# Output projection kept in the PSUM bank of the weighing for its last eleven steps

## The reference, cut to what matters

```
x = x + attention(layernorm(x), wq, wk, wv, wo)    # 32 query heads, 8 key/value heads of 64, rope, causal
x = x + cross(layernorm(x), ctx)                   # fp8-rounded in blocks of 128, one product per batch
x = x + moe(layernorm(x), Wg, W1, W3, W2, shared)  # 8 experts, top 1, capacity 256, and a shared expert
```

## Time and profile before

| | |
|---|---|
| median of three timed runs | 1606.17 us (1605.36 to 1607.48) |
| profiled execution, its own time | 1609.08 us |
| its span | 1607.3 us |
| PE busy | 1460.3 us, 91% of the span |
| DVE busy | 1202.9 us, 75% |
| POOL busy | 1020.0 us, 63% |
| ACT busy | 949.2 us, 59% |
| the profiled steps 124 to 134 | from about 999 us to about 1079 us |

### The profile page before, as it was taken

The page is one execution under the profiler, slowest core; times in us unless marked ns, Lnnn a source line. Parts: engine busy times, 40 slices in busy tenths (PEclk is TensorE's granted clock), DMA queues, the critical chain, the costliest instruction groups (busy, mean ns, idle before and its releaser), DMA issues.

```text
span 1607.3 us, 26926 instructions
## 1 busy us (share of the span) xinstructions
PE 1460.3 (91%) x8616; PEld 1276.6 (79%) x8616; DVE 1202.9 (75%) x2951; ACT 949.2 (59%) x2384; POOL 1020.0 (63%) x1007
## 2 busy tenths in 40 slices
PE   5689899999998999999999998666989898899997
PEld 4468788888877888888888887556888887899996
DVE  6678688888877778877878878976767664687785
ACT  2367677877766687878877877523121213566662
POOL 1677688988966788888888877632313132344455
PEclk8899999999999999999999999897899999899998
DMA  5654243344332334334334433012010002577767
GB/s 195 179 157 148 61 116 112 85 120 125 81 104 50 78 86 126 91 93 120 99 93 112 110 79 109 14 55 86 27 27 27 7 27 97 175 232 224 229 215 236
DMA packets 106588, 177.04 MB, mean 110 GB/s; under 512 B 16662, under 2 KB 38422, under 8 KB 106448
## 3 DMA queue, kind: packets, MB, share of 16 engines
q1 hardware_dynamic: 103888, 167.07, 35.9%
q0 software_dynamic: 2560, 8.25, 1.6%
HBM read 97.28 MB, written 31.98 MB: 80 GB/s over the span
## 4 chain that ended last, share of the span: by engine, by line
PE 66%; DVE 15%; ACT 7%; issue 5%; POOL 3%; DMA 2%; SPq 1%; DVEq 0%; POOLq 0%; ACTq 0%
PE bank L411 14%; PE bank L412 14%; PE bank L413 14%; PE bank L453 6%; PE bank L429 4%; PE bank L468 4%; PE bank L469 4%; PE bank L430 4%; ACT P L756 3%; PE bank L403 2%; DVE P L1033 2%; DVE Opair L1068 1%; ACT xnx L778 1%; ACT Otmp L762 1%; DVE work L981 1%
## 5 line engine op out<-in xcount | busy, mean ns | idle before, releaser
L756 ACT ACTIVATE P<-P,mn 128x512 f32<-128x512 f32 (+3 forms) x512 | 284.9, 557 | 220.7 <-DVE mn L1033 217.1
L1440 POOL TENSOR_TENSOR P<-P,ri 128x128 f32<-128x128 f32 (+3 forms) x512 | 358.9, 735 | 38.1 <-DVE ri L1022 31.1
L1033 DVE CUSTOM_DVE_ANT_0 P<-bank,mask 128x512 f32<-128x512 f32 (+3 forms) x512 | 236.3, 480 | 111.7 <-PE bank L430 109.3
L1074 DVE TENSOR_TENSOR PTl<-bank,PTh 128x512 fp32r<-128x512 f32 (+1 forms) x384 | 229.4, 598 | 32.9 <-ACT PTh L768 30.4
L429 PE MATMUL bank<-KT,QT 128*128 128x256 f32 (+2 forms) x512 | 190.2, 372 | 24.2 <-DVE mn L1033 23.2
L453 PE MATMUL bank<-ident,P 128*128 128x128 f32 x1280 | 203.3, 274 | 1.1 <-POOL P L1440 1.1
L768 ACT ACTIVATE PTh<-bank 128x512 fp32r<-128x512 f32 (+1 forms) x384 | 197.5, 515 | 5.6 <-PE bank L453 2.7
L411 PE MATMUL bank<-XT,Wh 128*128 128x512 f32 x384 | 165.2, 430 | 12.0 <-DVE qcs L1046 6.9
L468 PE MATMUL bank<-PTh,VS 128*128 128x256 f32 (+2 forms) x512 | 163.2, 329 | 13.3 <-DVE PTl L1074 8.6
L430 PE MATMUL bank<-KT,QT 128*128 128x256 f32 (+2 forms) x512 | 167.1, 326 | 0.0
L469 PE MATMUL bank<-PTl,VS 128*128 128x256 f32 (+2 forms) x512 | 156.5, 327 | 0.0
(11 more groups left out here) (194 smaller groups left out, 4226.0 us busy)
## 6 DMA issues: line engine op xcount, KB each, us to landing
RW<-in_wf SPq DMA_DIRECT2D x170, 256.0 KB, 3.2
QT<-qh SPq DMA_DIRECT2D x256, 64.0 KB, 2.0
QT<-ql SPq DMA_DIRECT2D x256, 64.0 KB, 2.0
Oraw<-in_wo SPq DMA_DIRECT2D x16, 512.0 KB, 5.1
xnx<-in_ctx SPq DMA_DIRECT2D x32, 256.0 KB, 3.5
KT<-KT SPq DMA_DIRECT2D x32, 256.0 KB, 3.0
Wraw<-in_wqkv SPq DMA_DIRECT2D x9, 768.0 KB, 4.7
saved<-Wh SPq DMA_DIRECT2D x7, 768.0 KB, 3.9
```

What stands on the lines that cost most here:

```text
L756: e.activation(pq, pq, ACT.Exp, bias=mn[:, z, qb:qb + 1], scale=-1.0, accum_out=rs[:, z, qb:qb + 1]).then_inc(a_exp, 1)
L1033: e.tensor_tensor_reduce(P[:, z, off[qb]:off[qb] + k], bank[n % 2][:, 0:k], mask[:, 512 - k:512], -0.125, BIG, ALU.add, ALU.min, mn[:, z, ...
L1074: e.tensor_tensor(pt_part(PTl, part), bank[2 + part][:, 0:128 * n].rearrange("p (m n) -> p m n", n=128), pt_part(PTh, part).bitcast(F32), ...
L1440: e.tensor_tensor(pq, pq, ri[:, z, qb:qb + 1].to_broadcast([128, n]), ALU.mult).then_inc(g_norm, 1)
```

## The change

The outputs 117 to 127 are written to bank 5 as all the others are, and wait as the others do. The exception is gone from `attn_out` on TensorE and on DVE, and from `wait_bank5`:

```
         def wait_bank5(need, h, user):
             if user == "attn_out":
-                need.wait_ge(a_tmp, h - 2)
-                need.wait_ge(v_join, h - 2)
+                need.wait_ge(a_tmp, min(h - 2, NH))
+                need.wait_ge(v_join, min(h - 2, NH))
+                if h - 3 >= NH:
+                    need.wait_ge(v_x, h - 7)
...
-            elif h < 8 or h - 8 >= NH - 11:
+            elif h < 8:
                 need.wait_ge(a_tmp, h - 3)
                 need.wait_ge(v_join, h - 3)
...
             else:
                 need.wait_ge(v_x, h - 7)

             def attn_out(n):
-                late = n >= NH - 11
-                ps = bank[7 if late else 5][:, :]
+                ps = bank[5][:, :]
...
-                if not late:
-                    wait_bank5(need, n + 7, "attn_out")
-                elif n == NH - 11:
-                    wait_part(need, NU - 1, 2)
-                else:
-                    need.wait_ge(v_x, n)
+                wait_bank5(need, n + 7, "attn_out")
```

More of the change, by code:

```diff
@@ L1082, in attn_out @@
                     need.wait_ge(v_x, n - 7)
-                e.tensor_tensor(X[:, t, :], X[:, t, :], bank[7 if n >= NH - 11 else 5][:, :], ALU.add).then_inc(v_x, 1)
+                e.tensor_tensor(X[:, t, :], X[:, t, :], bank[5][:, :], ALU.add).then_inc(v_x, 1)
             def scales(amax, r, d, least):
```

## The result

The changed kernel takes 1615.22 us (median of 13 runs, 1609.95 to 1620.85); the kernel before, on the same chips, 1607.63 us (13 runs, 1604.69 to 1611.96). The ratio is 1.0049, with a 95% interval of 1.0037 to 1.0061: 5.9 to 9.8 us slower, where 6.8 us were predicted. The time itself was forecast as 1613.0 us, on a kernel before of 1606.17; the measured 1615.22 stands on one of 1607.63, so 1.5 of the 2.2 us between them are the starting point's.

What follows compares the result with a forecast made beforehand. Two thirds of the kernel's chain was TensorE; in the changed stage DVE led first, then TensorE and both in turn. Terms 2.26 + 1.77 + 2.77 = 6.8 us, added to 1606.17, gave 1613.0 us, range 1609.0 to 1616.5.

Steps and rivals of the forecast that it cites:

- The path: Chain on DVE in steps 124 to 129, on TensorE from head 127's weighing; up to step 123 nothing moves.
- The clock at the outputs 118 and 120: Steps 124 to 127: both outputs run at 1.2 GHz after long idles, 1.13 us each, 2.26 taken; bounds 0 and 2.26.
- the outputs 117 and 119: Steps 124 to 127: gaps of some 1.8 to 2.6 us ahead of these outputs, given no cost.
- The idle ahead of output 120: TensorE waiting for the join, from 1031.2 or later to 1035.8: at most 4.6 us.
- Steps 128 to 130: No scores between an output and the next weighing, so added waits delay head 127's weighing: +1.77 us.
- the cross add moves by +0.76: Step 129: the later weighing of head 126 delays the first cross product's add on DVE by 0.76 us.
- Output 123's wait: Step 130's end: output 123 must wait for the join of head 127 on DVE, +2.77 us, the largest term.
- The sum: Added waits over the whole changed stretch, steps 124 to 134: 6.8 us slower.
- A: Outputs 118 and 120 keep 2.4 GHz, so 2.26 goes and 4.5 us are left: 1610.7 us; chance 0.24.
- B: TensorE's idle at the weighings absorbs the added waits, no cost: 1606.2 us; chance 0.11.
- C: The clock also falls in the tail, at the new gap before output 123, 1.7 us more: 1614.7; chance 0.14.
- D: Output 127 and 1093 to 1103 run at 2.4 GHz, 5.3 us back, not slower: 1605.4; chance 0.04.

Runs made afterwards that it cites:

- first experiment: Only outputs 117 to 120 put in bank 5, against the kernel before: ratio 1.0014 (1.0002 to 1.0026).
- sixth experiment: Changed kernel with the join of head 127 moved to the front of step 130 on DVE: ratio 1.0028 to the kernel before.
- second experiment: Only outputs 121 and 122 put in bank 5, against the kernel before: ratio 1.0019 (1.0009 to 1.003).
- fifth experiment: Changed kernel with filler matmuls ahead of each of the outputs 117 to 123 (all gaps filled): ratio 1.0039 to the kernel before.
- the fourth: Changed kernel with filler matmuls ahead of outputs 118 and 120 only (two gaps filled): ratio 1.0068 to the kernel before.
- output 123 alone: Only output 123 put in bank 5, against the kernel before: ratio 1.0024 (1.0013 to 1.0035).

## Why the prediction was right

**The path.** The rows behave as forecast: the steps up to 123 lie 0.45 us later and are the same within 0.02, DVE carries the chain to step 128 except where it waits for an output, and the delays add up to the last add.

**The clock at the outputs 118 and 120**: 2.26 forecast. The first experiment has 2.19 for the four outputs together, and the changed kernel less the one with all gaps filled 2.29. The choice between the ends (0 and 2.26) was right for both profiles of the changed kernel, and the outputs 117 and 119 were rightly given nothing there.

That it fits so well is in part luck. The sixth experiment, the same up to step 129, lost 1 us more at output 119. The idle ahead of output 120 was to be at most 4.6 us and was 5.31, since the sum left out that output 118's own loss puts the next joins off (the one of step 127 stands 38.54 us after output 116 and not 37.44) while TensorE ends its earlier work as early as before. And the idles by which the choice was made (2.19 kept the clock, 3.37 and 4.95 lost it) were not all: in the kernel before the weighing of head 123 starts at 1.2 GHz behind idles of 2.12, 0.67 and 0.68 us with four matmuls among them.

```profile
1017.21 0.76 PE L468 MATMUL bank<-PTh,VS 128*128 128x512 f32 x1 [0.68 <-ACT PTh L768]
```

**Steps 128 to 130**: 1.77 forecast, 2.05 measured in the second and in the fifth experiment. Here a size was off, and it is the step "the cross add moves by +0.76" that missed: it reckoned TensorE's side alone and let DVE's own work between the add of output 121 and the cross add keep its 5.05 us (1045.79 to 1050.84). In the second experiment, without any clock in play, that work took 5.80 us (1045.32 to 1051.12), so the cross add came 1.03 us late. The next join follows it on DVE, and the 0.27 us too few (1.03 less 0.76) are the miss of the whole term. Its two adds:

```profile
1045.32 0.69 DVE L1089 TENSOR_TENSOR X<-X,bank 128x512 f32<-128x512 f32 x1 [0.17 <-PE bank L420]
...
1051.12 0.68 DVE L1165 TENSOR_TENSOR X<-X,bank 128x512 f32<-128x512 f32 x1
```

What grew is the first piece of the rounding. The timelines of DVE and then of POOL, first of the kernel before, then of the second experiment (L987 and L1484 there are L981 and L1478):

```profile
1046.38 0.63 DVE L981 TENSOR_SCALAR work<-X,mv,rstd 128x512 f32<-128x512 f32 x1
```

```profile
1046.69 1.47 POOL L1478 TENSOR_TENSOR OTl<-Opair,OTh 128x512 fp32r<-128x512 f32 x1
```

```profile
1045.93 1.61 DVE L987 TENSOR_SCALAR work<-X,mv,rstd 128x512 f32<-128x512 f32 x1
```

```profile
1045.97 1.29 POOL L1484 TENSOR_TENSOR OTl<-Opair,OTh 128x512 fp32r<-128x512 f32 x1
```

Before, DVE's operation started 0.31 us ahead of POOL's and took 0.63 us, and POOL's took 1.47. Now that the add of output 121 is later, DVE's starts only 0.04 us ahead; POOL's takes 1.29, and DVE's 1.61. The Trainium skill, "SBUF — State Buffer", section "Who interferes with whom", has it as a rule: DVE in a two-port mode and GpSimd lock the shared ports for a whole instruction, and whoever comes first blocks the other. The profile names no mode, but the trace agrees in the durations: the engine that is held up is POOL before and DVE now, by 0.98 us, of which 0.24 came back at a short operation behind it (0.41 us before at L1086, 0.17 now). That POOL got the ports first is read from these durations and not from the starts, which still have DVE ahead by 0.04; the profile's spans on POOL are rough. It is no chance of one execution. In the changed kernel's two profiles and in the second, fifth and sixth experiments, in which output 121 waits, POOL's start is 0.04 to 0.09 us behind DVE's and DVE takes 1.61 to 1.65; in the six kernels in which output 121 does not wait it is 0.31 to 0.34 behind, and DVE takes 0.63 to 0.66. (In the fourth, where output 121 ran at the lower clock, POOL's had started 1.22 us ahead and DVE took 0.54.)

**Output 123's wait**: 2.77 forecast, 2.73 to 2.75 measured in the three executions that kept the clock there (the changed kernel twice, all gaps filled); all of it goes when the join is moved.

**The sum**: 6.8 forecast, 7.0 in the stretch of two profiles, and 5.9 to 9.8 in the timed runs. The profiled span grew by 4.0 us only (1607.3 to 1611.3). That is not a smaller cost: the first expert product still stands 7.20 us later. These are the transposes ahead of it and its first matmul, before and after:

```profile
1093.53 1.94 PE L403 MATMUL bank<-ident,XN 128*128 128x128 f32 x8 [13.96 <-DVE XT L1154]
...
1096.92 0.55 PE L411 MATMUL bank<-XT,Uh 128*128 128x256 f32 x1 [1.46 <-ACT XT L802]
```

```profile
1100.72 1.94 PE L405 MATMUL bank<-ident,XN 128*128 128x128 f32 x8 [13.58 <-DVE XT L1150]
...
1104.12 0.55 PE L413 MATMUL bank<-XT,Uh 128*128 128x256 f32 x1 [1.46 <-ACT XT L798]
```

The 3.2 us were regained behind it, where this execution had the clock up more. The windows of 303 us behind the first expert product, of the kernel before, of the changed kernel and of its second profile:

```profile
1097.00:1400.00 303.00, 269.55 (x1701) 243.49 (x1702) 194.58 (x480) 79.00 (x172) 78.88 (x65) 0.92 0.17 54
```

```profile
1104.00:1407.00 303.00, 267.52 (x1720) 242.30 (x1721) 194.35 (x481) 81.25 (x177) 78.28 (x66) 0.94 0.17 56
```

```profile
1103.00:1406.00 303.00, 269.32 (x1700) 243.23 (x1701) 194.56 (x480) 79.11 (x172) 77.98 (x65) 0.92 0.17 54
```

The second profile, with 0.92 there, took 510.06 us from the first expert product to the end of its span, as the kernel before did (510.4); the first took 507.2. That the clock made the difference is argued from these windows and was not tested.

**The rivals.** A (the clock holds, 4.5 us) is what the kernel with all gaps filled shows, at 4.7. B (slack swallows it) is refuted: each part alone costs. With it falls the reading of the Trainium skill, "TensorE: Matmul & The Clock Gate", section "HAM oscillation — how this bites in real kernels", by which adding PSUM double-buffering "gave no further gain": what that page measured on another kernel does not hold for this one, whose second bank is worth 4.7 us by the waits alone. C did happen with output 123 alone and with two gaps filled, not in the profiles of the changed kernel. Whether it is what makes its slowest runs was not seen; of the timed executions only the mean clock is known, and it is 0.958 in the slowest (1620.85 us) and 0.969 in the fastest (1609.95). D fell: the low clock before the experts stayed, 1.94 us for the same eight transposes.

## What to carry to other kernels

Two users that take turns in one PSUM bank cost nothing while an engine's own work covers the handovers. Once that work ends their round trip (join, output, add, weighing) lies in the chain: here 2.05 us for two outputs and 2.75 for one; so look at the last steps of a pipeline by themselves, where a free bank is worth most. When a wait is added, look in the order of the releasing engine: here it was the instructions ahead of the join, not the join, that made 2.7 of 7 us, and moving one call removed them. Before calling a few microseconds a loss or a gain, compare from a point just ahead of the change to one just behind it, since the rest of the program, which is the same in all these kernels, took from 506.4 to 510.4 us in the profiles without fillers there.

## What the runs showed of the hardware that I had not expected

Filling two idle gaps of TensorE, where the clock had fallen, did not save time but made the one profiled execution 3.9 us longer there: the low clock moved to matmuls behind gaps of 2.53, 2.87 and 3.23 us. The same gap of 2.53 us ahead of output 123 was followed by 0.47 us matmuls at 2.4 GHz in both profiles of the changed kernel, by 0.76 at once in the kernel with two gaps filled, and by a fall within the output in the kernel with output 123 alone. So in this kernel the length of a single gap doesn't always say whether the clock falls, and filling some gaps changes others: ahead of output 119 TensorE idled 2.10 to 2.29 us and kept the clock in the first experiment and both profiles of the changed kernel, and idled 3.22 and 3.23 us and lost it in the sixth and fourth experiments. Only filling all of them (0.47 at each of the outputs 117 to 123, granted clock 1.00 over 82 us) kept it.

The meeting of DVE and POOL is the other surprise: a delay of 0.28 us in an add went with 0.75 us more for DVE in what follows, because an operation that had held up POOL's `OTl` was now held up itself.
